# A vision tower on one core: two attention layers put into one program each, sparse softmax partly on ScalarE, a rearranged scan start and expert loop

## The reference

```python
top_k = int(0.4 * tgt_len)                       # 14 of 36
kth = jax.lax.top_k(attn_weights, top_k)[0][..., -1:]
sparse = jnp.where(attn_weights >= kth, attn_weights, min_val)
attn = softmax(sparse)
out = attn @ v
```

## Time and profile before

| what | value |
|---|---|
| runs shown | 944.35, 948.4, 944.51 us; median 944.51 |
| the profiled execution | 950.86 us, its span 949.0 us |
| PE busy | 840.1 us (89%), 6257 matmuls |
| PEld busy | 682.3 us (72%) |
| DVE busy | 396.7 us (42%) |
| ACT busy | 303.6 us (32%) |
| POOL busy | 291.6 us (31%) |
| mean granted TensorE clock | 0.907 of 2.4 GHz |

### The profile page before, as it was taken

How to read it: one execution, slowest core, us unless ns; L and a number is a source line. 1 busy time by engine, 2 the same in 40 slices (tenths; PEclk the granted TensorE clock), 3 DMA queues, 4 the chain that set the end, 5 groups by cost and what they waited for, 6 DMA issues and landing times. The chain is left out here.

```text
span 949.0 us, 18563 instructions
## 1 busy us (share of the span) xinstructions
PE 840.1 (89%) x6257; PEld 682.3 (72%) x6257; DVE 396.7 (42%) x1184; ACT 303.6 (32%) x633; POOL 291.6 (31%) x321
## 2 busy tenths in 40 slices
PE   8996999899989869999979999999789959889891
PEld 6775988565666449997548999999455847688881
DVE  1353222323451347886572222222152883444443
ACT  2430222215343066663301222222224223334340
POOL 0013555100020137771123444444110000247772
PEclk9987999988888979999779999999899778789995
DMA  9616989200000142210165898989813300658885
GB/s 358 255 43 211 304 259 301 69 1 1 1 2 0 38 167 77 73 40 1 40 218 160 314 299 303 323 279 300 240 44 121 111 2 18 184 166 263 255 266 167
DMA packets 56443, 148.84 MB, mean 157 GB/s; under 512 B 7952, under 2 KB 18944, under 8 KB 55872
## 3 DMA queue, kind: packets, MB, share of 16 engines
q1 hardware_dynamic: 47296, 125.10, 39.4%
q0 software_dynamic: 9088, 22.98, 8.7%
HBM read 134.58 MB, written 13.47 MB: 156 GB/s over the span
## 5 line engine op out<-in xcount | busy, mean ns | idle before, releaser
L1554 POOL DMA_INDIRECT L_xr<-x_rows_L,L_rows_in x92 | 93.9, 1021 | 40.3 <-issue 33.6
L2357 DVE TENSOR_TENSOR L_act<-L_hid,bank 116x512 f32<-116x512 f32 (+1 forms) x56 | 35.9, 640 | 160.8 <-ACT L_hid L2326 90.3
L2246 POOL DMA_INDIRECT y_rows_L<-L_yb,L_rows_out x56 | 55.8, 996 | 106.6 <-ACT L_yb L2332 97.3
L2326 ACT ACTIVATE L_hid<-bank 116x512 f32<-116x512 f32 (+1 forms) x56 | 31.3, 559 | 167.3 <-PE bank L2296 157.3
L2290 PE MATMUL bank<-L_xtb,L_w 128*116 128x128 f32 (+1 forms) x464 | 57.8, 278 | 0.1
L2290 PEld LDWEIGHTS bank<-L_xtb,L_w 128*116 128x116 f32 (+1 forms) x464 | 55.0, 187 | 0.7 <-issue 0.6
L2306 PE MATMUL bank<-L_w,L_act 116*128 116x192 f32 (+1 forms) x232 | 46.1, 340 | 2.7 <-ACT L_yb L2332 2.7
L1461 POOL TENSOR_TENSOR ssm_w_low<-ssm_wbc,ssm_w_high 128x512 fp32r<-128x512 f32 x24 | 31.4, 1310 | 42.5 <-ACT ssm_w_high L1419 42.5
L1620 POOL TENSOR_TENSOR L_s_up<-L_s_hid,L_s_up 116x288 f32<-116x288 f32 (+1 forms) x10 | 7.9, 794 | 114.6 <-ACT L_s_up L1614 114.6
L2290 PE MATMUL bank<-L_xtb,L_more 128*116 128x128 f32 (+1 forms) x352 | 42.7, 273 | 0.0
L2306 PEld LDWEIGHTS bank<-L_w,L_act 116*128 116x128 f32 (+1 forms) x232 | 36.8, 189 | 6.7 <-ACT L_yb L2332 2.9
(11 more groups left out here) (460 smaller groups left out, 1888.1 us busy)
## 6 DMA issues: line engine op xcount, KB each, us to landing
L_w<-in_L2w SPq DMA_DIRECT2D x20, 696.0 KB
L_more<-in_L2w SPq DMA_DIRECT2D x20, 696.0 KB
L_w<-in_L2w SPq DMA_DIRECT2D x20, 384.0 KB
L_more<-in_L2w SPq DMA_DIRECT2D x20, 384.0 KB
L_w<-in_L0w SPq DMA_DIRECT2D x12, 576.0 KB
L_more<-in_L0w SPq DMA_DIRECT2D x12, 576.0 KB
ssm_wbc<-in_wBC SPq DMA_DIRECT2D x24, 256.0 KB
L_w<-in_L3w SPq DMA_DIRECT2D x16, 384.0 KB
```

The source lines that it names most:

```text
L1554: pool.indirect_dma_start(self.xr[j][:, :], None, self.x_rows[:, :], bass.IndirectOffsetOnAxis(ap=at, axis=0))\
L2246: pool.indirect_dma_start(X.y_rows[:, :], bass.IndirectOffsetOnAxis(ap=rows_out[h][:, j:j + 1], axis=0), y[s + j][:, :], None).then_inc(st ...
L2326: act.activation(hid[j][:, :, :], cols(gate_bank[j % 2][0:N, 0:C * R], C), ACT.Silu).then_inc(acted, 1)
L2357: dve.tensor_tensor(act_out[j][:, :, :], hid[j][:, :, :], cols(up_bank[j % 2][0:N, 0:C * R], C), ALU.mult)\
```

## The change

Layer two's three blocks become one, as do layer four's. A function `ready`, handed from the projections to the attention, makes PE and POOL wait for what the block's end stood for; the output projections wait for `att_in` by halves. Buffers of layer two now share space. POOL's four selection operations wait until the norm of the feed-forward is done. In the sparse attention, for groups 0, 1 and 2, DVE no longer subtracts the maxima and no longer multiplies by 1 / sum: it negates the maxima, and ACT makes 16 Exp of 108 x 36 with the negated maximum as bias, and later 16 scaled copies of 108 x 36 with 1 / sum as scale; group 3 stays as it was. In the scan ACT does the norm before the two casts, the second feature plane goes first, Ln is done in two halves with the sum on DVE behind each, the Exp table is loaded ahead, tile 0's `grown` is made by DVE in one operation, and PE gets two `wake` matmuls (four instructions) before the tiles. The inner loop of layer three's experts gets five turns in place of four. The last `wake` of both tails is one matmul in place of two. `linear`, `residual` and `biased` go.

```diff
-    "L2": dict(experts=128, top=6, pairs=6, cap=192, width=464, chunks=4, group=4, ...
+    "L2": dict(experts=128, top=6, pairs=6, cap=192, width=464, chunks=4, group=5, ...
...
 head_attention
+    early = BATCHES - 1 if sparse else 0
     @block.gpsimd
     def _(pool):
+        ready(pool, True)
         pool.memset(padded[:, :, SEQ:TALL], 0.0).then_inc(cleared, 1)
     @block.tensor
         for g in range(BATCHES):
+            ready(pe, g > 0)
...
         def turn(g):
-            pe.wait_ge(probs, g + 1)
+            if g < early:
+                pe.wait_ge(act_probs, g + 1)
+            else:
+                pe.wait_ge(probs, g + 1 - early)
...
         def exponentials(g):
             act.wait_ge(lowered, g + 1)
-            part = sc[:, CH * g:CH * g + CH, :]
-            act.activation(part, part, ACT.Exp).then_inc(exps, 1)
+            if g < early:
+                for i in range(CH * g, CH * g + CH):
+                    ins = act.activation(sc[:, i, :], sc[:, i, :], ACT.Exp, bias=mx[:, i:i + 1])
+            else:
+                part = sc[:, CH * g:CH * g + CH, :]
+                ins = act.activation(part, part, ACT.Exp)
+            ins.then_inc(exps, 1)
+        def scale(g):
+            if g < early:
+                act.wait_ge(inverted, g + 1)
+                for i in range(CH * g, CH * g + CH):
+                    ins = act.activation(sc[:, i, :], sc[:, i, :], ACT.Copy, scale=total[:, i:i + 1])
+                ins.then_inc(act_probs, 1)
         def take_turned(g):
+            scale(g)
...
         def lower(g):
...
-                    link(dve.tensor_copy(top, top8[:, CH * g:CH * g + CH, 0]))
+                    link(dve.tensor_scalar(top, top8[:, CH * g:CH * g + CH, 0], -1.0, None, ALU.mult))
...
-                dve.tensor_tensor(part, part, spread(top, 2, SEQ), ALU.subtract).then_inc(lowered, 1)
+            if g < early:
+                dve.sem_inc(lowered, 1)
+            else:
+                dve.tensor_tensor(part, part, spread(top, 2, SEQ), ALU.subtract).then_inc(lowered, 1)
...
         def normalize(g):
...
+            if g < early:
+                dve.reciprocal(tot, tot).then_inc(inverted, 1)
+                return
...
 head_projections
+    def ready(pe, banks):
+        pe.wait_ge(qk_in, 8)
+        pe.wait_ge(spread_q, 6)
+        if router:
+            pe.wait_ge(router.chosen, 4)
+        if banks:
+            pe.wait_ge(v_second_in, VU)
+    return ready
...
 feed_forward
         for s in range(2):
+            pe.wait_ge(att_in, 4 * s + 4)
...
     def _(pool):
+        pool.wait_ge(norm.normalized, 2)
         link(pool.tensor_scalar(inv[:, :, :], bits[:, :, :], -1.0, 1.0, ALU.mult, ALU.add))
...
 selective_scan, PE
             pe.wait_ge(relu_made, 2)
+            wake(T, T.bank[2 * SUM_AT], 2)
...
 selective_scan, ACT
+            norm.act(act)
             split_high(0)
             split_high(1)
-            norm.act(act)
...
-            act.activation(mag[:, :, :], mag[:, :, :], ACT.Ln, bias=1.0).then_inc(soft, 1)
-            split_high(2)
+            for m in (1, 0):
+                act.activation(mag[:, m, :], mag[:, m, :], ACT.Ln, bias=1.0).then_inc(soft, 1)
+            T.load_table(ACT.Exp)
...
 selective_scan, DVE, tile 0
+                    dve.wait_ge(decayed, 1)
+                    dve.scalar_tensor_tensor(grown[0][:, :], d[:, :], -1.0, xs[:, of(0), :], ALU.add, ALU.mult).then_inc(first_grown, 1)
...
 Tail.pe
-        wake(T, T.bank[7], BRIDGE)
+        wake(T, T.bank[7], BRIDGE // 2)
...
 layer3_attention
-        with nc.Block() as block:
-            head_projections(...)
-        head_attention(T, "a3_att", qk, wide, v, p["avb"], att, True, second)
-        linear(T, "a3_proj", 2, 2, ..., by_dve=residual(T, T.h, p["aprojb"]), size=128, bridge=BRIDGE // 2)
+        block = ctx.enter_context(nc.Block())
+        ready = head_projections(...)
+        att_in = head_attention(T, ctx, block, "a3_att", ready, qk, wide, v, p["avb"], att, True, second)
+            for s in range(2):
+                pe.wait_ge(att_in, 4 * s + 4)
```

More of the change, by code:

```diff
@@ L455, in wide_layer @@
[L455 removed]
+def wide_layer(T, ctx, block, name, norm, of, first_loads, w, qk_bias, wv, softmax_scale=None, linear_scale=None, v_bias=None, att_bias=None, proj=None, proj_bias=None, space=None):
     nc = T.nc
@@ L620, in wide_layer, with head_attention @@
     return h_in
-def head_attention(T, name, qk, wide, v, vb, att, sparse, also=None):
+def head_attention(T, ctx, block, name, ready, qk, wide, v, vb, att, sparse, also=None, space=None):
     nc = T.nc
@@ L830 @@
+    return att_in
 class SecondWeights:
@@ new lines, in _ @@
+        for s in range(2):
+            pe.wait_ge(down_in, 2 * s + 2)
+            for m in range(2):
+                for k, part in enumerate((d01, d2)):
+                    mm = pe.matmul(up_bank[s][m][:, 0:HALF], up[k][:, 128 * m:128 * m + 128], part[:, at(s)], start=(k == 0), stop=(k == 1))
+                mm.then_inc(up_made, 1)
+        wake(T, T.bank[0], BRIDGE // 2)
+    @block.scalar
+    def _(act):
+        norm.act(act)
+        for s in range(2):
+            for m in range(FC):
+                act.wait_ge(fc1_made, FC * s + m + 1)
+                act.activation(mid[:, m, at(s)], fc1_bank[s][m][:, 0:HALF], ACT.Gelu, bias=p["fc1b"][:, m:m + 1]).then_inc(mid_in, 1)
```

727 lines of the change are left out of this document (328 added, 399 removed).

## The result

The changed kernel takes 918.37 us (median of 4 runs, 915.25 to 920.16) beside 944.43 for the kernel before (4 runs, 944.01 to 948.40): a ratio of 0.971, 95% interval 0.967 to 0.975. Forecast were 924.0 and a gain of 20.5; measured are 26.1. The change makes the kernel faster, as said, and the gain is 5.6 us larger than said. The profiled execution took 920.16 us (span 918.4). A second comparison, six runs against eleven, gave 919.71 against 942.06, ratio 0.975 (0.972 to 0.978), a gain of 22.4.

The account below looks back on a forecast made before the run. PE is busy most of the span, DVE bounds layer four, and five places hold avoidable waits. Gains of 4.7 + 5.6 + 5.7 + 1.9 + 2.6 = 20.5 us take 944.51 to 924.0 us; range 918 to 932.

Parts of the forecast that it names:

- Pause behind the loop: Layer three, behind the expert loop: PE's idle time shrinks from 5.11 to 1.5 us as turns are skipped.
- the loop's edit: Layer three, five turns a group: 3.6 us from skipped turns and 2.1 from the clock behind them, sum 5.7.
- both meetings: Layers two and four: engines no longer meet ahead of scores (1.3 us) and ahead of output projection (1.03 us).
- the rival of no overlap: Layer four's softmax: each short ACT operation costs its whole 0.32 us, a batch 5.1; total 931.6 us; chance 0.09.
- the one in which they are run one by one: Layer four's softmax: 96 short ACT operations each wait for the one before, 0.54 us each; total 949.2; chance 0.02.
- 1.1 in the scan: Scan's first four tiles: 1.1 us gained from PE's clock and the earlier start, with `wake` filling some of the pause.
- 2.1 in the tail of layer three: Behind layer three's loop: the first ten PE instructions run at the higher clock, 2.6 us in place of 4.70.
- it comes back in more places: Rival: higher clock also in the scan, group 2's transposes and layer two's feed-forward; gain 24.8, 919.7 us; chance 0.13.
- The scan's 5.6: Scan: tile 0's drive comes 4.5 us earlier, and the first four tiles gain 1.1 us; bounds 4.5 and 6.5.
- The tails' 1.9: Two tails: one `wake` matmul fewer in each, 0.9 us apiece, since everybody waits for them; no fall of the clock.
- Sparse softmax 0.3: Layer four: softmax work moved to ACT lets group 2's transposes come 1.5 us earlier, 1.3 of it the block's end.
- the 2.4 of my sum: Layer four's softmax: time taken for turn 0 with its copies between ACT's batches, some 2.4 us of 24.4.

Follow-up runs that it names:

- `pool_first`: The changed kernel with layer two's four GpSimd selection operations at the head of GpSimd's feed-forward program, without the wait for the norm: 923.46 us, 3.7 slower.
- the second profile of the kernel before: The kernel before, with no edit, profiled once more: 943.15 us, span 941.4.

## Why the prediction was right or wrong

**Right:** the direction, and the mechanisms with their sizes where no clock is in them. Pause behind the loop 1.57 (said 1.5), loop 3.7 us (3.6), tail with wake 2.8 (3.05); alone and undone the loop's edit gave 5.5 and 5.3 (5.7). Additions at 0.46 us once GpSimd waits; both meetings gone in both layers. Short operations on ACT 0.22 us apart and 3.55 a batch (3.6), and with them the rival of no overlap fell, and the one in which they are run one by one.

**Wrong, in the sum.** The failed step is the clock's. I priced it only where the edits remove a pause (1.1 in the scan, 2.1 in the tail of layer three) and put it at nothing elsewhere: behind the tails because the wait there stays as long, but in layer two and ahead of layer four's scores without a reason. The case that came, "it comes back in more places", got 0.13, and came at other places than the feed-forward and the transposes that I had named. What the runs showed in its place: 2.9 us beyond the meeting in the linear attention, 1.1 in layer two's softmax and 2.8 ahead of layer four's scores, and 1.9 less than forecast in the scan, whose norm now ran at the lower clock. Half of the time that the lower level lost in the first three places (6.8, 3.4 and 6.8 us) would be 3.4, 1.7 and 3.4; so half the low time is a fair upper estimate.

These gains are not all the change's. The 2.9 us came in two variants of the kernel before as well (59.4 and 59.3 us), and were gone again, in whole or in part, in four of the changed one (67.6 to 69.3 us from layer two's norm to the scores, against 64.8). The softmax's 1.1 are steadier: it took 22.1 us in all six profiles of kernels with the meetings, 19.8 to 20.0 in all that are merged, but for `pool_first`. What moves the low stretches stays open.

**How the miss adds up.** The result is 5.6 us beyond the forecast. 2.4 of it is the kernel before, which took 944.43 in the first comparison and 942.06 in the second; 1.3 is the changed kernel between the same two (918.37, 919.71); 1.9 is left for the stages. My base of 944.51 was the median of three runs; comparisons of eleven gave 942.0, 942.1, 942.8 and 941.3, and the fourth, of 25, gave 947.6.

**The scan's 5.6** was right for the edit and wrong for the sum: 5.8 by the stage when undone, with drive 0 4.8 earlier (said 4.5); 7.4 alone, where the low clock went too; but 3.7 from kernel to kernel, since the norm's first matmuls ran at the lower clock (3.87 us in place of 2.18). That their earlier arrival did this is likely and not shown. The two `wake` matmuls, for which I took some of the 1.1, do nothing for the scan.

**The tails' 1.9** is nearly right as the wakes' own time (0.86 us each by the traces; the prediction's own product, 0.92, makes 1.8 when doubled) and wrong as an effect: undone 4.6, alone a loss of 2.7.

**Sparse softmax 0.3:** -0.3 by the traces, with the attention at 48.5 us when it is undone and 48.8 with it. I had left out that group 0's transposes wait for ACT's scaling, which puts 5.27 us of pause and a low clock where there was 0.46 us. They took 3.20 us, so turn 0 with its copies stood between ACT's batches for 3.7 us and not for the 2.4 of my sum. The Trainium skill's rule on large tiles (Advanced Engine Details and Errata, The Read-Write Bubble) spoke against this part. The trace bore its cost out: 3.55 us where one operation takes 0.67. I had said that it falls on an engine that waited. That held only in part: the layer got no slower, but one batch fewer on ACT made the attention 4.7 us shorter, so the cost had reached the end.

## What to carry to other kernels

Price an edit by what it removes, but in a kernel whose PE clock falls some twenty times, add a few us of either sign to every sum: the low stretches lay at other places when PE came a little earlier or later, and now and then in another execution of the same code. An edit tried alone, or undone, then gives its own cost plus that. Judge such edits by several executions and read the stage, not the total. When work goes to an idle engine, walk the chain once for each group: the group for which the other engine is idle at that moment should stay there, which was worth more than the move itself (4.3 us against nothing). And when blocks are merged, ask which engine now runs ahead into whose time.

## What the runs showed of the hardware

**PE's clock.** One and the same stretch of code, linear attention to scores, took 62.8, 62.3, 59.4, 59.3 and (with a shorter wake ahead) 65.5 us in five profiles, with 17, 17, 10, 10 and 24 us at the lower level; half the difference of these accounts for the times within 1 us. The Trainium skill (TensorE: Matmul & The Clock Gate, Part 1) states that what sets the clock's level runs freely and doesn't start with the kernel, so that one kernel measures different numbers of slow matmuls; the traces agree. The Trainium skill puts, in the same part, the loss by the ramp to the higher clock under 1% of a typical span and advises against fitting a number of slow matmuls. This case is about later falls: some twenty an execution, 134 to 193 us at the lower level of spans of 908 to 953, up to half of it lost where PE is the bound, and they made up several of the differences told above. The clock also fell in the midst of PE's work, not only behind its pauses: in the second profile of the kernel before, PE's scores of layer two ran from 248.1 on without idle time, and the clock fell at 251.6 (0.77 over that attention, with PE busy 20 of 22 us).

**DVE beside GpSimd.** A DVE operation with two SBUF inputs of 576 columns took 1.18 in place of 0.76 us while GpSimd's two-input operations ran, and those took 1.80 to 1.92 in place of 1.40; DVE's reductions beside them stayed at 0.74. The Trainium skill (SBUF — State Buffer, Who interferes with whom) names the same pairs, those with two SBUF inputs against GpSimd reading SBUF, and leaves reductions out: the traces agree. The Trainium skill there calls the contention an exclusive lock, and the rows of `pool_first` fit that: the one that comes second waits for the rest of the first one's instruction. GpSimd's instructions had 0.57, 0.28 and 0.57 us left when DVE's three began, and DVE lost 0.42, 0.14 and 0.42; in the kernel before 0.92 were left at 275.25, and 0.78 lost:

```profile
274.77 1.40 POOL L1242 TENSOR_TENSOR b_sel<-b_inv 64x576 f32<-64x576 f32 x1
```

It is the same the other way: DVE's operation of 250.86 had 0.54 left at 251.22, and GpSimd lost 0.40. Each time the loss is some 0.15 us less than the rest.
